# One-hot sums of the message layer: float32r operands and two 12-bit parts in place of bfloat16 and three parts

## What is computed

```python
x_j = node_features[col]                                    # col = dst
m = einsum('ei,ej,ijh->eh', x_j, edge_attr, W_msg_tp) * norm   # per edge, 16 values
m = silu(m)
m = m @ W_msg_lin * norm_lin
agg = segment_sum(m, row, num_segments=n_nodes)             # row = src, not sorted
...
```

## Time and profile before

| what | before |
|---|---|
| device time, median of 3 runs | 23584.9 us (23537.7 to 23600.5) |
| profiled execution, first to last instruction | 23516.1 us |
| message stage: POOL's first scatter to the next stage's first load | 15422.2 to 19420.0 us |
| POOL busy / PE busy / DVE busy in 16000 to 19000 us | 2538 / 2864 / 1720 us |
| scatters in the stage, mean busy time, idle before each | 2000, 1.675 us, 0.30 us |
| one-hot matmuls in the stage | 13500 |

### The profile page before, as it was taken

The page is one execution under the profiler, slowest core; times in us unless marked ns, Lnnn a source line. Parts: engine busy times, 40 slices in busy tenths (PEclk is TensorE's granted clock), DMA queues, the critical chain, the costliest instruction groups (busy, mean ns, idle before and its releaser), DMA issues. The chain is left out here.

```text
span 23516.1 us, 304821 instructions
## 1 busy us (share of the span) xinstructions
PE 18959.3 (81%) x105910; PEld 12094.2 (51%) x105910; DVE 13526.5 (58%) x25320; ACT 2368.9 (10%) x5716; POOL 17392.8 (74%) x15021
## 2 busy tenths in 40 slices
PE   0688882789995388888888888679999998899997
PEld 0344441344442255555555555367777765555556
DVE  2788883455554266666556555445555552677772
ACT  0000000000000011111111111011111111111111
POOL 5777774777775788888888888478888880777775
PEclk9888885899997688888888888779999997999998
DMA  2222221112121111111222111123333321788884
GB/s 96 51 61 61 61 60 20 40 42 47 41 47 27 27 32 32 32 32 32 35 37 36 32 32 30 30 53 47 52 49 48 50 34 54 236 251 251 250 250 127
DMA packets 1968267, 1657.06 MB, mean 70 GB/s; under 512 B 780455, under 2 KB 1732934, under 8 KB 1949718
## 3 DMA queue, kind: packets, MB, share of 16 engines
q0 software_dynamic: 889216, 465.71, 14.3%
q10 hardware_dynamic: 821300, 579.22, 7.9%
q1 hardware_dynamic: 256354, 594.03, 7.5%
HBM read 953.63 MB, written 684.18 MB: 70 GB/s over the span
## 5 line engine op out<-in xcount | busy, mean ns | idle before, releaser
L1347 PE MATMUL node_sums<-placed_row,lane_values 128*128 128x392 bf16 x34500 | 6165.9, 338 | 534.3 <-DVE placed_row L1335 534.3
L1405 POOL DMA_INDIRECT acc<-column_sums,sum_rows x3375 | 5663.3, 1678 | 1193.1 <-issue 1140.1
L803 POOL DMA_INDIRECT gathered<-gat_table,src_index x4810 | 4835.3, 1005 | 1496.3 <-issue 1471.0
L1347 PEld LDWEIGHTS node_sums<-placed_row,lane_values 128*128 128x128 bf16 x34500 | 3455.8, 102 | 2962.7 <-DVE placed_row L1335 557.2
L1626 POOL DMA_INDIRECT gathered<-sheaf_table,src_index x3125 | 3402.1, 1089 | 960.2 <-issue 942.9
L2409 POOL DMA_INDIRECT gathered<-message_table,src_index x2381 | 2362.0, 992 | 727.5 <-issue 725.1
L1010 PE MATMUL lanes_ps<-S,table_parts 128*128 128x512 bf16 x9828 | 2272.4, 394 | 334.3 <-DVE S L875 334.3
L1335 DVE TENSOR_SCALAR placed_row<-iota_rows_f,src_row 128x1568 bf16<-128x1568 f16 x2875 | 1799.7, 651 | 1119.5 <-PE node_sums L1347 1090.3
L1010 PE MATMUL lanes_ps<-code_onehot,table_parts 128*128 128x512 bf16 x9828 | 2210.5, 386 | 154.7 <-DVE code_onehot L875 154.5
L1010 PEld LDWEIGHTS lanes_ps<-S,table_parts 128*128 128x128 bf16 x9828 | 985.3, 102 | 1558.3 <-DVE S L875 320.3
L1010 PEld LDWEIGHTS lanes_ps<-code_onehot,table_parts 128*128 128x128 bf16 x9828 | 972.5, 100 | 1332.3 <-DVE code_onehot L875 161.9
(11 more groups left out here) (484 smaller groups left out, 22192.5 us busy)
## 6 DMA issues: line engine op xcount, KB each, us to landing
message_rows<-gathered ACTq DMA_DIRECT2D x250, 1600.0 KB, 11.4
src_rows<-src_rows SPq DMA_DIRECT2D x200, 640.0 KB
src_rows<-src_rows SPq DMA_DIRECT2D x125, 960.0 KB
code_rows<-src_code_rows SPq DMA_DIRECT2D x360, 256.0 KB, 3.3
gat_rows<-scanned ACTq DMA_DIRECT2D x25, 3375.0 KB
gathered<-gat_table,src_index POOLq DMA_INDIRECT x4810
acc<-column_sums,sum_rows POOLq DMA_INDIRECT x3375, 3.1
gat_rows<-scanned ACTq DMA_DIRECT2D x25, 2125.0 KB, 6.8
```

The source lines that it names most:

```text
L803: g.indirect_dma_start(G[b][:, j, :], None, tab, bass.IndirectOffsetOnAxis(ap=IX[b][:, j:j + 1], axis=0)).then_inc(s_g[b], 16)
L1347: last = pe.matmul(o.acc[:, m, 0:Q8 // 4], lane, o.OW[r][:, m * (Q8 // 4):(m + 1) * (Q8 // 4)], start=first(k, 1) and i == 0 and part == 0 ...
L1405: g.indirect_dma_start(self.acc[i], bass.IndirectOffsetOnAxis(ap=o.IXS[b][:, j:j + 1], axis=0), o.SV[b][:, j, :], None, compute_op=ALU.add ...
```

## The change

In the message layer alone, both operands of the one-hot sums become float32r (4 bytes in memory), and the values are split into two parts in place of three: the top 12 significant bits, by a mask on the bits, and the remainder. The one-hot row and `lane_values` are written as float32r, `tile_sum` makes 8 matmuls a column in place of 12, and `lane_values` takes 2 products a group in place of 3. The 45 columns, the buffers' counts, the order of the steps and the waits stay. The sheaf layer keeps bfloat16 and three parts through the defaults.

```diff
+R32 = mybir.dt.float32r
...
-    def tile_buffers(self, c, o, mt, onehot, lanes=2, io=None):
+    def tile_buffers(self, c, o, mt, onehot, lanes=2, io=None, parts=PARTS, dt=BF16):
...
-        o.SVH = [sb(f"lane_values{i}", [P, PARTS, ACCS, 8, D], BF16) for i in range(lanes)]
+        o.SVH = [sb(f"lane_values{i}", [P, parts, ACCS, 8, D], dt) for i in range(lanes)]
...
+    def split_wide(self, v, w, values, top, parts):
+
+        w(v.tensor_scalar(top.bitcast(I32), values.bitcast(I32), -4096, None, ALU.bitwise_and))
+        v.tensor_copy(parts[:, 0], top)
+        w(v.tensor_tensor(parts[:, 1], values, top, ALU.subtract))
...
-        for i in range(PARTS):
+        for i in range(o.parts):
             ins = v.tensor_tensor(o.SVH[r][:, i], bcast(o.E8[:, a:a + ACCS, :].unsqueeze(3), [P, ACCS, 8, D]),
...
-        for part in range(PARTS):
+        for part in range(o.parts):
             lane = o.SVH[self.lane_buffer(o, b, t)][:, part, i % ACCS].rearrange("p h d -> p (h d)")
...
-            parts = sb("value_parts", [P, PARTS, MT2, D], BF16)
+            top = sb("value_top", [P, MT2, D])
+            wide = sb("value_parts", [P, 2, MT2, D], R32)
+            parts = wide[:].bitcast(F32)
...
-            self.tile_buffers(c, o, MT2, [sb(f"placed_row{i}", [P, Q8], BF16)[:] for i in range(ACCS)], 2, keep[:])
+            self.tile_buffers(c, o, MT2, [sb(f"placed_row{i}", [P, Q8], R32)[:] for i in range(ACCS)], 2, keep[:], 2, R32)
...
-                            self.split(v, w, VT[:], parts)
+                            self.split_wide(v, w, VT[:], top[:], wide)
```

More of the change, by code:

```diff
@@ L1271, in equal @@
                         bcast(o.SRC[:, g * ACCS:(g + 1) * ACCS].unsqueeze(2), [P, ACCS, P]), ALU.is_equal).then_inc(o.s_eq, 1)
-    def tile_buffers(self, c, o, mt, onehot, lanes=2, io=None):
+    def tile_buffers(self, c, o, mt, onehot, lanes=2, io=None, parts=PARTS, dt=BF16):
         sb, sem = (lambda n, s, d=F32: self.sb(n, s, d, c)), (lambda n: self.sem(n, c))
-        o.mt, o.OW, o.ring, o.lanes = mt, onehot, len(onehot), lanes
+        o.mt, o.OW, o.ring, o.lanes, o.parts = mt, onehot, len(onehot), lanes, parts
         o.LOI = sb("src_bits", [P, mt], I32)
@@ L2111, in compute @@
                             v.wait_ge(s_vt, k * 2)
-                            self.split(v, w, VT[:], parts)
+                            self.split_wide(v, w, VT[:], top[:], wide)
                         else:
-                            v.sem_inc(s_v, 2 * PARTS - 1)
-                            w.n += 2 * PARTS - 1
+                            v.sem_inc(s_v, 2)
+                            w.n += 2
                         self.src_bits(v, w, o, srcc[:, SC:CH], b)
@@ L2145, in _ @@
                     last = Chain(v, s_v, w0.n + NCH * K[0])
-                    self.split(v, last, VT[:], parts)
+                    self.split_wide(v, last, VT[:], top[:], wide)
                     for i in range(MT2):
```

## The result

The changed kernel takes **23923.97 us** (median of 4 runs, 23904.32 to 23960.27). The kernel before, run beside it, takes 23592.61 us (4 runs, 23537.73 to 23600.48). The ratio is 1.0152, with a 95% interval of 1.0136 to 1.0167: **331 us slower**. The forecast said slower by 86, so the sign is right and the size is not: 23924 lies 134 us above the upper end of the range.

The account below looks back on a forecast made before the run. POOL's scatters were taken to bound the message stage. Delays +119 us and the stage's end -33 gave +86 on the span of 23516.1, and with 68.8 for the runs' median 23670 us; range 23460 to 23790.

Parts of the forecast that it names:

- POOL sets the pace: Message stage: POOL's 2000 scatters run without a pause, 1.675 us each and 0.305 us apart, 158.4 us a chunk.
- PE's relief is worth nothing: Message stage: 8 matmuls for 12 save PE 30 us a chunk, worth nothing since POOL never waits for PE.
- float32r runs at nearly bfloat16's pace: PE's one-hot sums: a float32r matmul of 392 columns takes 0.166 us, as in bfloat16.
- Rivals 3 and 4: PE's matmuls: float32r takes two cycles a column, 24300 us (11%); plain float32 in disguise, about 27270 us (4%).
- The one-hot row: DVE's 1125 rows of 128x1568, now 4 bytes an element, go from 0.635 to 0.976 us, taken from a cast.
- Rival 2: DVE's one-hot row runs at one element a cycle and leaves the port lock: 122 us less, 23463 us (8%).
- The end: Message stage's end: PE's last sums fall beside POOL's last chunk, 6 us behind POOL in place of 39.2, 33 less.
- Delays at the first place: POOL's scatters held by DVE instructions just after their start: 309 to 406 us against 239, taken as 119 more.
- the factor 0.76: POOL's delays before the change: 239 us measured against 315 by chance placing; applied to 406 it gives 309.
- a scatter needs something, once, just after its start: POOL's scatter waits until a DVE instruction running 0.13 us after its start ends; all delays, 239 us, were put there.
- The chance formula: POOL's delays with DVE instructions placed by chance: sum of N x (D - 0.1)^2 / 2T, 315 us before, 406 after.
- Rival 1: POOL's delays don't grow; only the stage's end counts: 23550 to 23590 us, no change (11%).

## Why the prediction was right in sign and wrong in size

- **POOL sets the pace: right.** Its gap stayed 0.305 us; in no kernel with 45 columns was a gap longer than 0.4 us once the first scatter had begun, but for a single one of 0.63 with two-operand rows.
- **PE's relief is worth nothing: right.** Eight matmuls bought 689 us in 3000 that PE now waits, behind `s_chunk` as forecast, some 39 us a chunk. With twelve matmuls again the kernel lost 302 us to before, with eight 331.
- **float32r runs at nearly bfloat16's pace: nearly right.** From the two rows of PE above, 8 more matmuls cost 3.11 - 1.68 us, 0.179 us each, against 0.166: 8% more, at a granted clock of 1.00 in both stretches. Rivals 3 and 4 (0.33 us and more) fall.
- **The one-hot row: nearly right.** 1.054 us measured, 0.976 taken from the cast. Some of it is the stretch that a row suffers inside a scatter, like the 1.19 above; undisturbed ones take 1.03 to 1.05. Rival 2 (1.7 us, out of the lock) falls.
- **The end: right.** 35 us less, 33 forecast.
- **Delays at the first place: nearly right, in part by luck.** Forecast were 309 to 406 in all, 358 in the middle; at that place the trace has 306. The low end of 309 rests on the factor 0.76, which took in the 30 us of the second place; the first place's own 202 us give 202 / 315 = 0.64, and 260 us.
- **The step that failed** is "a scatter needs something, once, just after its start". It needs it twice. The second need was in the rows of before, with 30 us in 126 scatters, and I took the delays of all kinds together as one sum of 239 and a factor, so that this was hidden in the factor. It grew to 313 us. The chance formula finds less than half of that. A row holds a scatter there if it has begun by 1.17 us and lasts past 1.47, which makes 1125 x (D - 0.3)^2 / 2T: before, 1125 x 0.335^2 / 3.96 = 32 us, where 30 were measured; after, with D = 1.05 and T = 1.867 + 0.305 = 2.17 us, 1125 x 0.75^2 / 4.34 = 146 us, where 313 were. The other half is where the rows stand, which is not chance. An instruction that holds a scatter's start lets it go as it ends; often a two-operand instruction of 0.82 us follows it, and then a row, which so begins 0.74 to 0.80 us into the scatter (counted, as the 1.17 and 1.47, from a start put later by the first delay). Before, 193 rows began there, 167 of them in that order, and ended at 1.43 us, just short of 1.47. After, 342 do, 317 in that order, and end at 1.84 us: all of them hold their scatter, 127 of the 313 us.
- **Rival 1** (the delays don't grow) falls with the 384 us. That the change does what it says is shown by its rows: 9000 float32r matmuls in the stage, 450 `lane_values`.

Not tried: a one-hot row of one element a cycle with a single tensor operand, and a row made by another engine than DVE. Where the other rows stand in their scatters, and why more of them begin between 0.42 and 1.17 us after the change (638 of 1125, 349 before), is shown by the traces but not explained.

## What to carry to other kernels

Where GpSimd's indirect DMAs pace a stage, the cost of a DVE instruction beside them grows faster than its length, and its kind says at how many places it counts: price each instruction that grows longer at each place before counting what another engine saves. With places by chance that is the square of the length (less what must pass before it holds) times N / 2T; it is an estimate, and the measured delays were 0.6 to 2.1 times it here, so look too at where the instruction stands in the scatter now, and what its new end will reach (1.43 us before, 1.84 after). Look in the trace for delays that a rule leaves unexplained, however small: 30 us in 126 scatters were the sign of what became 313. An instruction that holds a shared resource is better cut in pieces, even at more work in all, and a saving on an engine that isn't the bound is worth something only once work is moved to it (55 columns and halved rows: 269 us faster than before).

## What the runs showed that was not expected

- A scatter of 128 rows is held at two moments: by a DVE instruction that runs 0.13 us after its start, and by a one-operand one that has begun by about 1.17 us and lasts past 1.47. One-operand comparisons hold it at both, two-operand products at the first alone (804 of 816 us in the kernel with two-operand rows).
- Between the two, a two-operand instruction may begin and end freely; a one-operand row that begins 0.50 to 0.75 us into a scatter is itself lengthened, from 1.03 to as much as 1.34 us.
- A float32r row has a fixed part that pieces pay again: 1.054 us for 1568 elements and 0.431 for 392 (means, with what they suffer beside scatters) give 0.53 ns an element and 0.22 us besides. With the same fixed part the bfloat16 row of 0.64 us would make 0.27 ns an element, half as much, from the same float16 input.
- TensorE's granted clock fell from 0.96 to 0.85 with PE's pauses of some 40 us a chunk and rose to 0.97 when twelve matmuls filled them; since POOL paced the stage in both and its gaps stayed as they were, this cost nothing.
